# Third cross-attention on one core: variances of two chunks made and read together, the running maximum folded to 128 columns before the last chunk

## The reference

```python
kvx = jnp.einsum('bsi,oi->bso', cond, w_kv_x)           # cond: the 6272 context rows
kx, vx = jnp.split(kvx, 2, axis=-1)
kx = _ln(kx.reshape(b, sc, g, d), kxln_w, kxln_b)       # layer norm over each head's 128 values; g = 8 groups
vx = vx.reshape(b, sc, g, d)
xout = _gqa(qx, kx, vx)     # softmax(qx . kx / sqrt(128)) . vx, 2 query heads for each of the 8 groups
```

## Time and profile before

| | us |
|---|---|
| median of 3 runs | 1064.81 (1062.67 to 1066.28) |
| the profiled execution, its own time | 1061.59 |
| its span, first to last instruction | 1059.8 |
| PE busy | 994.1 (94% of the span) |
| DVE busy | 716.2 (68%) |
| ACT busy | 358.4 (34%) |
| POOL busy | 156.9 (15%) |

### The profile page before, as it was taken

The page is one execution under the profiler, slowest core; times in us unless marked ns, Lnnn a source line. Parts: engine busy times, 40 slices in busy tenths (PEclk is TensorE's granted clock), DMA queues, the critical chain, the costliest instruction groups (busy, mean ns, idle before and its releaser), DMA issues.

```text
span 1059.8 us, 20606 instructions
## 1 busy us (share of the span) xinstructions
PE 994.1 (94%) x7822; PEld 657.2 (62%) x7846; DVE 716.2 (68%) x1909; ACT 358.4 (34%) x627; POOL 156.9 (15%) x143
## 2 busy tenths in 40 slices
PE   6999999998789988899999999999999999988898
PEld 4776677675335544365777777677777777743455
DVE  3777767768779834787676767767676767743343
ACT  2332333334428721443333333333343332301211
POOL 0000000001000010233222323222222323000000
PEclk9999999999999999998999999999999999899999
DMA  7100101002229996860000000000000000232430
GB/s 284 41 22 22 38 20 40 20 5 96 99 62 188 192 313 217 320 241 2 1 1 1 1 0 0 0 0 0 0 0 0 0 1 2 79 140 88 174 159 4
DMA packets 68729, 76.09 MB, mean 72 GB/s; under 512 B 52544, under 2 KB 59456, under 8 KB 64832
## 3 DMA queue, kind: packets, MB, share of 16 engines
q1 hardware_dynamic: 68240, 74.71, 23.1%
q10 hardware_dynamic: 432, 0.62, 0.2%
HBM read 62.41 MB, written 0.07 MB: 59 GB/s over the span
## 4 chain that ended last, share of the span: by engine, by line
PE 73%; DVE 11%; issue 5%; DMA 4%; ACT 3%; POOL 3%; SPq 0%; DVEq 0%; POOLq 0%; PEldq 0%
PE ps L2215 15%; PE ps L2109 13%; PE ps L1480 8%; PE ps L2205 7%; PE ps L1470 4%; PE ps L1491 4%; PE ps L1514 2%; PE ps L1526 2%; POOL x_sum L2733 2%; ACT vals L2016 2%; DMA x_keys<-vals 2%; DVE S L2420 1%; PE ps L528 1%; PE ps L1874 1%; PE ps L2817 1%
## 5 line engine op out<-in xcount | busy, mean ns | idle before, releaser
L2215 PE MATMUL ps<-vals,S 128*128 128x257 f32 x784 | 188.5, 384 | 0.7 <-ACT S L2665 0.7
L2109 PE MATMUL ps<-keysT,row_biases_sb 128*128 128x512 f32 (+1 forms) x416 | 186.3, 573 | 1.0 <-DVE row_biases_sb L2094 0.9
L2733 POOL TENSOR_TENSOR x_sum<-x_max,consts 128x4 f32<-128x4 f32 (+1 forms) x104 | 133.6, 1285 | 322.4 <-DVE x_max L2408 322.4
L2420 DVE SCALAR_TENSOR_TENSOR S<-ps,x_sum,keysT 128x128 f32<-128x128 f32 x392 | 110.9, 344 | 73.3 <-PE ps L2215 64.2
L2215 PEld LDWEIGHTS ps<-vals,S 128*128 128x128 f32 x784 | 143.3, 192 | 19.0 <-issue 1.0
L2665 ACT ACTIVATE S<-S 128x512 f32<-128x512 f32 (+1 forms) x104 | 62.7, 606 | 219.1 <-DVE S L2455 218.5
L2205 PE MATMUL ps<-x_q,x_keys 128*128 128x128 f32 x784 | 114.2, 288 | 0.0
L2109 PEld LDWEIGHTS ps<-keysT,row_biases_sb 128*128 128x128 f32 x416 | 76.6, 192 | 57.7 <-issue 52.6
L2205 PEld LDWEIGHTS ps<-x_q,x_keys 128*128 128x128 f32 x784 | 96.4, 193 | 0.0
L1480 PE MATMUL ps<-ring,S 128*128 128x512 f32 x196 | 92.2, 593 | 0.5 <-DVE ps L1621 0.5
L2597 ACT COPY x_keys<-ps 128x512 f32<-128x512 f32 (+1 forms) x104 | 57.1, 549 | 67.5 <-PE ps L2109 34.3
(11 more groups left out here) (453 smaller groups left out, 1366.1 us busy)
## 6 DMA issues: line engine op xcount, KB each, us to landing
ring<-weights SPq DMA_DIRECT2D x24, 1024.0 KB, 5.9
keysT<-ctxT SPq DMA_DIRECT2D x2, 3136.0 KB, 14.9
vals<-ctxN SPq DMA_DIRECT2D x1, 6272.0 KB, 24.3
S<-ctxT SPq DMA_DIRECT2D x12, 512.0 KB, 4.1
ring<-weights SPq DMA_DIRECT2D x6, 768.0 KB, 7.1
keysT<-weights SPq DMA_DIRECT2D x1, 1792.0 KB, 8.8
keysT<-weights SPq DMA_DIRECT2D x1, 1536.0 KB, 12.0
row_biases_sb<-row_biases SPq DMA_DIRECT2D x1, 1416.0 KB, 12.0
```

Source lines behind the costliest of these rows:

```text
L2109: ins = pe.matmul(ps[:, x2_key_bank(g, c), 0:width(c)], x2_wk[:, k, :], ctxT[:, k, span(c)], start=k == 0, stop=k == KT - 1)
L2215: ins = pe.matmul(bank(6, D + 1), S[:, a:a + TILE], ctx_and_ones[:, SUB * c + s, :], start=c == 0 and s == 0, stop=c == NC - 1 and s == su ...
L2420: ins = dve.scalar_tensor_tensor(S[:, a:a + TILE], ps[:, 3 + c % 2, 128 * s:128 * s + 128], x2_inv[:, c % 2, s:s + 1], x2_tile_const, ALU. ...
L2733: pool.tensor_tensor(x2_inv[:, c % 2, 0:n], x2_var[:, c % 2, 0:n], C("neg_half").broadcast_to([128, n]), ALU.pow)\
```

## The change

It does two things. Variances of chunks 1 and 2, 3 and 4, up to 11 and 12 are made by TensorE in one go and read by VectorE in one instruction of 8 columns, and inverted by GpSimd in one instruction of 8 columns; chunk 0 stays alone. So a group has 7 reads and not 13. TensorE does them in even chunks: at chunk c the variances of c+1 and c+2. For that, `low_half(c + 2)` moves on VectorE ahead of `running_max(c)` in even chunks. The other thing: at chunk 11 two maxima fold the running maximum from 512 to 128 columns (`fold_running`), and the 128 scores of chunk 12 are then compared straight into the result; `top_of_lanes` goes.

```diff
-            def variance(g, c):
-                pe.wait_ge(sem("x2_square_low"), g * NC + (c + 1))
-                if c >= 1 or not (isinstance(g, int) and g == 0):
-                    pe.wait_ge(sem("x2_var_read"), g * NC + c)
-                for s in range(subs(c)):
...
+            def variance(g, r):
+                chunks = X2_TOGETHER[r]
+                pe.wait_ge(sem("x2_square_low"), g * NC + (chunks[-1] + 1))
+                if r >= 1 or not (isinstance(g, int) and g == 0):
+                    pe.wait_ge(sem("x2_var_read"), g * X2_READS + r)
+                for c in chunks:
+                    for s in range(subs(c)):
...
+                        if c % 2 == 0 and c + 2 < NC:
+                            variance(scored, c // 2 + 1)
                         if c + 1 < NC:
-                            variance(scored, c + 1)
                             scores(scored, c + 1)
...
+            def read_var(g, r):
+                dve.wait_ge(sem("x2_keys_var"), g * NC + (X2_TOGETHER[r][-1] + 1))
+                if r >= 1 or not (isinstance(g, int) and g == 0):
+                    dve.wait_ge(sem("x2_inverse"), g * X2_READS + r)
+                n = SUB if r == 0 else 2 * SUB
+                dve.tensor_scalar(x2_max[:, 0:n], ps[:, 7, 0:n], LN_EPS, None, ALU.add).then_inc(sem("x2_var_read"), 1)
...
+                if c == NC - 1:
+                    dve.wait_ge(sem("x2_running"), g * X2_RUNS + X2_RUNS)
+                    dve.tensor_tensor(x2_lanes_top, x2_running[:, 0:128], S[:, span(c)], ALU.max).then_inc(sem("x2_max"), 1)
+                    return
...
-                dve.tensor_reduce(x2_lanes_top, x2_running.rearrange("p (s r) -> p r s", s=SUB), AX, ALU.max).then_inc(sem("x2_max"), 1)
+            def fold_running(g):
+                for i, n in enumerate((256, 128)):
+                    dve.wait_ge(sem("x2_running"), g * X2_RUNS + (NC - 1 + i))
+                    best = x2_running[:, 0:n]
+                    dve.tensor_tensor(best, best, x2_running[:, n:2 * n], ALU.max).then_inc(sem("x2_running"), 1)
...
-                    if scored is not None and c + 1 < NC:
-                        read_var(scored, c + 1)
+                    if scored is not None and c % 2 == 0 and c + 2 < NC:
+                        low_half(scored, c + 2)
                     if scored is not None:
                         running_max(scored, c)
+                    if scored is not None and c == NC - 2:
+                        fold_running(scored)
                     if weighed is not None and c >= 1 and c + 2 < NC:
                         shift(weighed, c + 2)
-                    if scored is not None and c + 2 < NC:
+                    if scored is not None and c % 2 == 0 and c + 2 < NC:
+                        read_var(scored, c // 2 + 1)
+                    if scored is not None and c % 2 == 1 and c + 2 < NC:
                         low_half(scored, c + 2)
...
-                pool.tensor_tensor(x2_inv[:, c % 2, 0:n], x2_var[:, c % 2, 0:n], C("neg_half").broadcast_to([128, n]), ALU.pow)\
+                n = SUB if r == 0 else 2 * SUB
+                pool.tensor_tensor(x2_sum[:, 0:n], x2_max[:, 0:n], C("neg_half").broadcast_to([128, n]), ALU.pow)\
```

More of the change, by code:

```diff
@@ L2060, in perceiver @@
         x2_block_heads = (x2_qx_heads[:, 0:512], x2_qx_heads[:, 512:1024], x2_q_heads[:, 0:512], x2_q_heads[:, 512:1024], x2_k_heads)
+        X2_TOGETHER = [(0,)] + [(c, c + 1) for c in range(1, NC, 2)]
+        X2_READS = len(X2_TOGETHER)
+        x2_read_of = lambda c: (c + 1) // 2
+        X2_RUNS = NC + 1
         x2_running = wide[:, 2, :]
@@ L2178, in core_out @@
                 ins.then_inc(sem("x2_core_out_psum"), 1)
-            def variance(g, c):
-                pe.wait_ge(sem("x2_square_low"), g * NC + (c + 1))
-                if c >= 1 or not (isinstance(g, int) and g == 0):
-                    pe.wait_ge(sem("x2_var_read"), g * NC + c)
-                for s in range(subs(c)):
-                    a = SUB * (c % 2) + s
-                    tile_of = slice(TILE * s, TILE * s + TILE)
-                    pe.matmul(ps[:, 7, a:a + 1], high_half(c)[:, tile_of], x2_mean, start=True, stop=False)
-                    ins = pe.matmul(ps[:, 7, a:a + 1], x2_low[c % 2][:, tile_of], x2_mean, start=False, stop=True)
-                ins.then_inc(sem("x2_keys_var"), 1)
+            def variance(g, r):
[5 more added lines that the diff above has]
+                    for s in range(subs(c)):
+                        a = SUB * (c % 2) + s
+                        tile_of = slice(TILE * s, TILE * s + TILE)
+                        pe.matmul(ps[:, 7, a:a + 1], high_half(c)[:, tile_of], x2_mean, start=True, stop=False)
+                        ins = pe.matmul(ps[:, 7, a:a + 1], x2_low[c % 2][:, tile_of], x2_mean, start=False, stop=True)
+                    ins.then_inc(sem("x2_keys_var"), 1)
             def scores(g, c):
@@ L2398, in low_half @@
                    .then_inc(sem("x2_square_low"), 1)
[L2400 to L2408 removed]
+            def read_var(g, r):
[4 more added lines that the diff above has]
+                dve.tensor_scalar(x2_max[:, 0:n], ps[:, 7, 0:n], LN_EPS, None, ALU.add).then_inc(sem("x2_var_read"), 1)
             def scale(g, c, weighed):
                 dve.wait_ge(sem("x2_scores_psum"), since("x2_scores_psum", g * NC + (c + 1)))
[L2413 removed]
+                dve.wait_ge(sem("x2_inverse"), g * X2_READS + (x2_read_of(c) + 1))
                 if c == 0:
@@ L2429, in running_max @@
                 else:
-                    dve.wait_ge(sem("x2_running"), g * NC + c)
+                    dve.wait_ge(sem("x2_running"), g * X2_RUNS + c)
                     best = x2_running[:, 0:width(c)]
@@ L2470, in change @@
             def change(scored, weighed, ahead):
-                if scored is not None:
-                    top_of_lanes(scored)
                 if ahead is not None:
@@ L2724, in x2_pool, with inverse @@
             pool.memset(ctx_and_ones[:, :, D:D + 1], 1.0).then_inc(sem("untold"), 1)
-            def inverse(g, c):
-                pool.wait_ge(sem("x2_var_read"), g * NC + (c + 1))
-                if c >= 2:
-                    pool.wait_ge(sem("x2_scores"), since("x2_scores", g * NC + (c - 1)))
-                elif c == 0 and not (isinstance(g, int) and g == 0):
-                    pool.wait_ge(sem("x2_scores"), since("x2_scores", g * NC))
-                n = subs(c)
-                pool.tensor_tensor(x2_inv[:, c % 2, 0:n], x2_var[:, c % 2, 0:n], C("neg_half").broadcast_to([128, n]), ALU.pow)\
+            def inverse(g, r):
+                pool.wait_ge(sem("x2_var_read"), g * X2_READS + (r + 1))
+                if r >= 1 or not (isinstance(g, int) and g == 0):
+                    pool.wait_ge(sem("x2_scores"), since("x2_scores", g * NC + X2_TOGETHER[r][0]))
+                n = SUB if r == 0 else 2 * SUB
+                pool.tensor_tensor(x2_sum[:, 0:n], x2_max[:, 0:n], C("neg_half").broadcast_to([128, n]), ALU.pow)\
                     .then_inc(sem("x2_inverse"), 1)
@@ L2739, in x2_pool @@
                     .then_inc(sem("x2_block_inverse"), 1)
-            for c in range(NC):
-                inverse(0, c)
+            for r in range(X2_READS):
+                inverse(0, r)
             with pool.Fori(1, GROUPS) as g:
-                for c in range(NC):
-                    inverse(g, c)
+                for r in range(X2_READS):
+                    inverse(g, r)
         STAGES[6] = (x2_tensor, x2_vector, x2_scalar, x2_pool)
```

11 lines of the change are left out of this document (removed).

## The result

The changed kernel takes 1082.41 us (median of 4 runs, 1080.10 to 1085.28) where the kernel before takes 1063.74 (4 runs, 1062.65 to 1066.28) beside it: ratio 1.0173, 95% interval 1.0141 to 1.0205. It is slower by 18.7 us. Forecast were 1085.4 and a range of 1073 to 1106.

The account below looks back on a forecast made before the run. PE was taken to bound the third cross-attention's loop, so any PE wait adds time; 13.4 (steps 1 to 6) + 1.9 (step 7) + 5.3 (step 0) = 20.6 us on the median 1064.81 gave 1085.4, range 1073 to 1106.

Parts of the forecast that it names:

- Steps 1 to 6: Six repeating steps of the third cross-attention's loop: 2.23 us longer each, 13.4 in all.
- part A: Pair's variance in full even chunks: PE waits 0.33 us for the low half, five times, 1.65 per step.
- Part B: Chunk 10, with no keys left as cover: PE waits for chunk 12's low half, +1.64 us per step.
- Part C: End of the group: the 0.46 us stall before the transposing of the maximum goes; VectorE's path shortens by 0.89.
- Part D: Odd chunks: scores directly behind keys take 0.10 us less than behind a variance, six times, -0.60 per step.
- Step 7: Last step, no next group's keys to hide behind, so VectorE's chain counts whole: +1.9 us.
- Step 0: First step, without weighing, set by the ring and the clock: +5.3 us, between 1.9 and 9.5.
- the ring: Step 0's cycle through VectorE, PE and GpSimd: 7.1 us per pair of chunks, was 5.80, inverse at 1.95.
- The end path: Step 0 from the scaling of chunk 10 to the transposing of the maximum: 8.8 us, +0.4 on the old.
- Weight loads pay: Rival: idle weight loads, 0.57 us per variance visit, are PE time that fewer visits give back; 1065.6, not slower, chance 0.08.
- Only chunk 10 waits: Rival: the low half is in time in full chunks, so part A goes; 9.1 us slower, 1074, chance 0.08.
- The clock falls in each step: Rival: chunk 10's wait drops PE to 1.2 GHz, costing 3.35 us per step; 1105, chance 0.22.

Follow-up runs that it names:

- e4: The changed kernel with the low half of chunk 12 moved behind the maximum and shift of chunk 10; 1096.57 us, ratio 1.0295.
- e8: The changed kernel with PE making the odd chunk's scores before the pair's variance, VectorE's order unchanged; 1065.53 us, ratio 1.0022.
- e3: The changed kernel with pairs kept but the old reduction at the group's end in place of the folds; 1083.22 us, ratio 1.0175.
- e13: The changed kernel with chunks 11 and 12 single, low halves of even chunks and of chunk 11 earlier, pair's read directly behind the scaling; 1056.71 us, ratio 0.9929.
- e14: The kernel before with only the fold of the running maximum added, measured a second time; 1059.51 us, ratio 0.9957.
- e2: The kernel before with only the fold of the running maximum added, variances one chunk at a time; 1060.72 us, ratio 0.9957.
- e7: The changed kernel with, in even chunks, the low half ahead of the scaling and the variance read directly behind it; 1065.82 us, ratio 1.0024.
- e1: The changed kernel with, in even chunks, the low half of chunk c+2 ahead of the scaling of chunk c; 1077.25 us, ratio 1.0117.

## Why the prediction was right

**What bounds the kernel.** Right. VectorE's work begins 0.20 after PE's weighing ends (593.52 to 593.72), and e4's 1.01 of wait for 1.01 of time shows that PE's waits count whole. "And not earlier" holds, "in every chunk" does not: in e8 VectorE is still busy at chunk 10 and starts 0.42 behind.

**Steps 1 to 6.** Forecast +2.23 each, measured +2.37 in steps 2 to 6 and +2.59 in step 1. By terms: part A 0.33, measured 0.34, five times: 1.70. Part B 1.64, measured 1.66. Part C -0.46, measured -0.46 (by e3 the pairs bring it without the fold). Part D -0.60, measured six times 0.09, -0.53. The sum, 2.37, is the measured step to 0.01. From the weight-load rule of the Trainium skill (TensorE: Matmul & The Clock Gate, The mechanism) I had drawn that D would be zero; 0.89 against 0.97, the 1.82 in e8 and the 0.44 between e13 and e14 decide against a D of zero. They do not test the rule itself. That it is a first weight load which is hidden was my reading; the runs show only that the work behind a variance pays.

**Step 7.** Forecast +1.9, measured +2.2. From the scaling of chunk 11 to the transposing it is 4.14 before, 3.56 with the pairs alone (e3) and 3.28 with both, so the 0.89 of part C is 0.86: 0.58 for the wait for GpSimd that the pair takes away, and only 0.28 for the fold, which agrees with the 0.27 of e3's step. This split holds with the pairs in; without them, in e2, the fold alone takes 0.92 off this step (58.46 to 57.54). With the terms measured in step 2 the sum is 1.70 + 1.66 - 0.86 - 0.45 = 2.05. The 0.17 that is missing stands in PE's timeline of step 7:

```profile
879.35 1.88 PE L2114 MATMUL ps<-keysT,row_biases_sb 128*128 128x512 f32 x4
881.43 0.18 PE L2195 MATMUL ps<-sw_value_part,wide 128*128 128x1 bf16 x1 [0.20 <-DVE sw_key_out L2405]
```

From keys to variance it is 2.08 and not 2.06, in all five even chunks, so part A is 0.37 each, 1.83 in all, and chunk 10's wait is 1.69. With these the sum is 2.21. Step 1 has the same 2.08, which is part of its 0.22; why these two steps differ stays open.

**Step 0, the term that was mis-sized.** Forecast +5.3, measured +2.9. From chunk 4 to chunk 10 the ring cost 2.9 more (17.54 before, 20.44 after) where I had 3 x 1.3 = 3.9: the inverse took 1.63 and not 1.95. Before chunk 4 it was 0.5, not 1.0. The end path took 7.9 (489.97 to 497.91), not 8.8: the clock fell as forecast, but it was back at 495, and the eight keys took 4.28, not 6.88. How long it stays low is no constant of the place: some 3.4 us in this step 0, 6.7 in the kernel before and about 7 in e13, and no run shows what sets it. The slope that gave 1.95 came from inverses of 4 columns and of 1 that both ran beside VectorE's maximum; e7's 2.02 beside a maximum, against 1.63, is close to my 1.95. In the changed kernel the read stands behind the maximum, and no maximum runs beside it. So my number was that of another order. The Trainium skill (GPSIMD Engine Reference, 3.1 Elementwise — side-by-side cycle accounting) would have the columns nearly free; with VectorE idle, 4 took 1.01 (chunk 0 of step 0) and 8 take 1.63 here, so four more columns cost 0.62, and the trace does not agree.

**Outside.** The loop began 3.1 later and the work behind it took 1.9 less, which no step of the change touches, and both lie within the scatter of the traces. With step 0 at 2.4 too much and steps 1 to 7 at 1.4 too little, the total of 20.8 hit the forecast of 20.6 better than its parts did: that closeness is luck. The medians are 18.7 apart.

**The rivals.** "Weight loads pay" has a visit to the variance cost something, which is so, and the wrong size: 0.09 per visit and not 0.57. "Only chunk 10 waits" falls with the five gaps of 0.34. "The clock falls in each step" fell for this kernel, but the mechanism is real: behind waits that show 1.71 to 1.74 (e1) the clock fell in three steps and stayed in two, behind 2.45 to 2.51 (e4) it fell in three steps of seven. What decides between two steps with the same wait stays open, and the length of the wait alone does not: the 1.50 of the changed kernel left the clock up in all seven steps, and 1.47 in step 0 of the kernel before was followed by the fall. One of my arguments against this rival does not hold, that the clock did not fall at once behind the 3.48 before 901.88: it is at 0.50 from about 903.2 to 910 there, and in e1 too the fall came 0.9 to 1.6 after the wait had ended. This rival, at 0.22, was the one that came nearest.

## What to carry to other kernels

Grouping small operations moves their inputs' deadline forward by a whole iteration; before grouping, list for each input where it is made and how much of another engine's work lies between that and its use, above all in the last iteration, where the covering work has run out. The saving itself was 0.09 per visit here, and one uncovered wait of 1.66 cost more than all of them, so take the grouping only where no wait results (e13), and leave the last groups single. When a wait is removed, look for the next releaser: here it had been done only 0.6 ahead of the first (611.98 against 612.56), ran through three other engines, and came later with the edit itself: in e1 the square of chunk 12 is done 1.44 behind the weighing of chunk 10 and not 0.66.
